# One full-width product for each expert's down-projection, order sums by accumulating transfers, and a new order of a VectorE step, in a fused attention and mixture-of-experts block

## What is computed

```python
# per batch row b: x 1024 x 256; sa, ca, ga, sb, cb, gb from silu(c) @ wmod
h = layernorm(x) * (1 + ca) + sa
q, k, v = split(h @ W_in.T)                       # 16 heads of 16
Tq, Tk = chebyshev(clip(q / 4)), chebyshev(clip(k / 4))        # 11 orders, 5 of them weighted
kv, ks = cumsum(Tk * v, tokens), cumsum(Tk.sum(-1), tokens)
out = (Tq * kv * beta).sum(orders) / ((Tq.sum(-1) * ks * beta).sum(orders) + 1e-7)
x = x + ga * (out @ W_out.T)
h = layernorm(x) * (1 + cb) + sb
w = sqrt(softplus(h @ routing_W.T + bias)) kept for the top 2 of 8 experts
x = x + gb * (shared(h) + sum_e w_e * (silu(h @ W1_e + b1_e) @ W2_e + b2_e))
```

## Time and profile before

| | us |
|---|---|
| median of 3 runs (lowest, highest) | 1087.46 (1085.91, 1087.97) |
| the profiled execution's own time | 1086.55 |
| its span, first to last instruction | 1084.9 |
| PE busy, DVE busy | 948.9, 947.9 |
| ACT busy, POOL busy | 472.5, 516.6 |
| step with p = 1 (465.9 to 526.2) | 60.3 |
| step with p = 0 (526.2 to 587.5) | 61.3 |

### The profile page before, as it was taken

How to read it: one execution, slowest core, us unless ns; L and a number is a source line. 1 busy time by engine, 2 the same in 40 slices (tenths; PEclk the granted TensorE clock), 3 DMA queues, 4 the chain that set the end, 5 groups by cost and what they waited for, 6 DMA issues and landing times.

```text
span 1084.9 us, 15500 instructions
## 1 busy us (share of the span) xinstructions
PE 948.9 (87%) x4889; PEld 678.4 (63%) x4889; DVE 947.9 (87%) x1465; ACT 472.5 (44%) x702; POOL 516.6 (48%) x615
## 2 busy tenths in 40 slices
PE   3864749998998989999999999898999999889996
PEld 3643436675756666675757576675757576656774
DVE  1498989999999999999999999999999999999432
ACT  4334335372635445362635444362635445441431
POOL 2032646646645546536645546536645445454210
PEclk9876869999999999999999999999999999999999
DMA  8100001020202002020202011020202010020211
GB/s 270 45 1 20 20 0 50 1 59 1 69 1 59 1 9 60 0 58 0 69 0 58 0 16 53 0 58 0 69 0 39 0 24 25 1 39 1 44 21 20
DMA packets 31517, 34.18 MB, mean 32 GB/s; under 512 B 1299, under 2 KB 30430, under 8 KB 31462
## 3 DMA queue, kind: packets, MB, share of 16 engines
q1 hardware_dynamic: 21410, 22.72, 6.3%
q0 software_dynamic: 8448, 8.39, 5.9%
q10 hardware_dynamic: 1604, 2.46, 0.7%
HBM read 16.77 MB, written 16.79 MB: 31 GB/s over the span
## 4 chain that ended last, share of the span: by engine, by line
PE 32%; DVE 30%; issue 18%; POOL 11%; ACT 3%; DVEq 1%; POOLq 0%; ACTq 0%
PE ring L1257 13%; PE acc L1394 7%; DVE feat L945 7%; PE tr L1342 4%; PE tr L1310 4%; DVE feat L966 3%; POOL feat L625 2%; DVE hid L1094 2%; DVE feat L962 2%; DVE feat L1004 2%; DVE feat L1001 2%; POOL ms L357 1%; PE tr L1248 1%; DVE route L1083 1%; PE cfb L1368 1%
## 5 line engine op out<-in xcount | busy, mean ns | idle before, releaser
L784 ACT ACTIVATE hid<-ring,b1row 128x512 f32<-128x512 f32 x144 | 98.6, 685 | 163.5 <-PE ring L1257 163.5
L630 POOL TENSOR_TENSOR feat<-feat 128x1024 f32<-128x1024 f32 x32 | 75.6, 2364 | 197.7 <-DVE feat L962 152.8
L1394 PE MATMUL acc<-w,hid 128*128 128x256 f32 x640 | 156.6, 392 | 0.0
L1394 PEld LDWEIGHTS acc<-w,hid 128*128 128x128 f32 x640 | 117.1, 191 | 28.0 <-issue 14.5
L945 DVE TENSOR_TENSOR_SCAN feat<-zero,carry,feat 128x512 f32<-128x512 f32 x80 | 113.1, 1453 | 0.0
L945 DVE TENSOR_TENSOR_SCAN feat<-zero,feat 128x512 f32<-128x512 f32 x80 | 109.9, 1413 | 0.0
L1094 DVE TENSOR_TENSOR hid<-hid,cfb 128x512 f32<-128x512 f32 x128 | 86.2, 673 | 25.7 <-PE cfb L1368 25.3
L1257 PE MATMUL ring<-n2H,w1H 128*128 128x512 f32 x288 | 101.9, 436 | 0.0
L1257 PE MATMUL ring<-n1H,winH 128*128 128x512 f32 x192 | 67.3, 433 | 38.7 <-ACT hid L784 24.9
L742 ACT ACTIVATE feat<-ring,bqkv 128x512 f32<-128x512 f32 x96 | 65.7, 686 | 71.5 <-PE ring L1257 71.5
L382 ACT ACTIVATE ntok<-xin,ms 128x256 f32 (+1 forms) x64 | 33.2, 589 | 138.5 <-POOL ms L361 138.5
(11 more groups left out here) (169 smaller groups left out, 2238.7 us busy)
## 6 DMA issues: line engine op xcount, KB each, us to landing
xin<-in_L_attn_x SPq DMA_DIRECT2D x16, 512.0 KB, 5.5
out<-x SPq DMA_DIRECT2D x16, 512.0 KB, 4.5
out<-fin POOLq DMA_DIRECT2D x16, 512.0 KB, 6.2
gates<-gate_rows SPq DMA_DIRECT2D x16, 128.0 KB, 4.8
feat<-in_L_wmod SPq DMA_DIRECT2D x1, 1536.0 KB, 14.1
feat<-in_L_attn_W_in SPq DMA_DIRECT2D x1, 768.0 KB, 9.5
const<-in_constants ACTq DMA_DIRECT2D x1, 690.5 KB, 4.3
fin<-in_constants ACTq DMA_DIRECT2D x1, 512.0 KB, 5.2
```

The lines of the kernel that those rows point to most:

```text
L630: g.tensor_tensor(f(W + 2 * n), f(W + 2 * n), f(W + 2 * n + 1), ALU.add).then_inc(added, 1)
L784: a.activation(hid[:, e % NG], ring[bank][:, :], ACT.Silu, bias=b1row[:, e:e + 1]).then_inc(ring_copied, 1)
L1394: last = mm(acc[t // 2][:, t % 2], x[:, t * P:(t + 1) * P], w[:, e // 2], start=False, stop=(e == E), skip_group_check=True)
```

## The change

1. All nine down-projections are one full-width float32 product for each token block; `w2` holds all nine weights, and `w2H`, `w2L`, `hidH`, `hidL`, ScalarE's four copies and VectorE's four subtractions of a step are gone.
2. The two GpSimd additions and one of the two VectorE additions of orders become three accumulating transfers from SBUF to SBUF (512 KB each, issued by GpSimd); the third waits for the first two, and VectorE's last addition waits for the third.
3. The order of VectorE's step is another, the carries are saved by three copies in place of five, `weigh(i, p, 3)` and `token_stats` come later, and the sums of order 4 before those of order 2.
4. On ScalarE the first normalisation and the squares of the next chunk change places; the powers on GpSimd move.
5. The softplus series has three instructions fewer.

```diff
-        w2 = sb("w2", [P, E // 2 + 1, D])
-        w2H = sb("w2H", [P, E // 2, D], f32r)
-        w2L = sb("w2L", [P, E // 2, D], f32r)
+        w2 = sb("w2", [P, NE, D])
...
                 c = number(i, p)
                 pool.wait_ge(odd_ready, 4 * c + 2)
-                ge(pool, numerator, 2 * c)
+                ge(pool, numerator, c)
                 g.tensor_tensor(f(W + 4), f(KT5), f(V0), ALU.mult).then_inc(weighted5, 1)
 
             def add_orders(i, p, n):
 
-                pool.wait_ge(products, ND * number(i, p) + 2 * n + 2)
-                g.tensor_tensor(f(W + 2 * n), f(W + 2 * n), f(W + 2 * n + 1), ALU.add).then_inc(added, 1)
+                c = number(i, p)
+                if n < 2:
+                    pool.wait_ge(products, ND * c + 2 * n + 2)
+                else:
+                    pool.wait_ge(added[0], 16 * c + 16)
+                    pool.wait_ge(added[1], 16 * c + 16)
+                into, of = ((W, W + 1), (W + 4, W + 3), (W, W + 4))[n]
+                pool.sem_inc(sum_begun, 1)
+                g.dma_start(f(into), f(of), accum_op=ALU.add).then_inc(added[n], 16)
...
                     add_orders(i, p, 0)
+                    add_orders(i, p, 1)
+                if st["second"]:
+                    exps(*later(i, p, -1))
+                if st["attn"]:
+                    add_orders(i, p, 2)
                 if st["norm"]:
                     inv_std(pool, 0, *later(i, p, 2))
                 if st["second"]:
-                    exps(*later(i, p, -1))
                     scores(*later(i, p, -1))
-                if st["attn"]:
-                    add_orders(i, p, 1)
-                if st["second"]:
                     split_weights(*later(i, p, -1))
                 if st["ffn"]:
...
                     act.wait_ge(clipped, 2 * c + q + 1)
+                    ge(act, summed, 2 * c - 1 + q)
                     if q == 0:
-                        ge(act, summed, 2 * c)
+                        ge(act, weighted, (ND - 1) * c)
+                        ge(act, weighted5, c)
+                    else:
                         ge(act, products, ND * c)
                     a.activation(f(s), f(x), ACT.Square).then_inc(squares, 1)
...
-                a.activation(hidH[:, :], hid[:, e % NG], ACT.Copy).then_inc(hidH_ready, 1)
...
-                if st["norm"]:
-                    normalise_first(act, *later(i, p, 2))
                 silu(5)
-                high(4)
                 copy("v0")
                 copy("v1")
                 silu(6)
+                if qkv:
+                    for which in range(3):
+                        square(*nxt, 0, which)
                 silu(7)
-                high(6)
+                if st["norm"]:
+                    normalise_first(act, *later(i, p, 2))
                 silu(8)
                 if qkv:
-                    for q in range(2):
-                        for which in range(3):
-                            square(*nxt, q, which)
+                    for which in range(3):
+                        square(*nxt, 1, which)
...
-            ORDERS = (0, 1, 3, 2, 4)
+            ORDERS = (0, 1, 3, 4, 2)
+
+            BY_WEIGHT = (0, 1, 3, 2)
+            NCARRY, CARRIED = 3, {0: 1, 1: 1, 3: 2, 4: 2, 2: 3}
...
+            def carry_over(i, p, k):
+
                 if p == 0:
-                    dve.wait_ge(scanned, ND * c + j + 1)
-                    v.tensor_copy(carry[:, n], feat[:, W + n, :, CT - 1]).then_inc(carried, 1)
+                    at, n, j = ((0, 2, 1), (3, 2, 3), (2, 1, 4))[k]
+                    dve.wait_ge(scanned, ND * number(i, p) + j + 1)
+                    v.tensor_copy(carry[:, at:at + n], feat[:, W + at:W + at + n, :, CT - 1]).then_inc(carried, 1)
...
-                dve.wait_ge(added, 2 * c + 1)
-                v.tensor_tensor(f(W), f(W), f(W + 4), ALU.add).then_inc(numerator, 1)
-                dve.wait_ge(numerator, 2 * c + 1)
-                dve.wait_ge(added, 2 * c + 2)
+                dve.wait_ge(added[2], 16 * c + 16)
                 v.tensor_tensor(f(W), f(W), f(W + 2), ALU.add).then_inc(numerator, 1)
...
-                for k, m in enumerate((11, 9, 7, 5, 3)):
-                    dve.wait_ge(soft_steps, at + 6 + k)
-                    v.scalar_tensor_tensor(out=b(PL), in0=b(PL), scalar=2.0 / m, in1=b(Z2),
+                v.scalar_tensor_tensor(out=b(PL), in0=b(Z), scalar=LOG1P[4], in1=b(Z),
+                                       op0=ALU.mult, op1=ALU.mult).then_inc(soft_steps, 1)
+                for k, m in enumerate((3, 2, 1)):
...
-                v.tensor_tensor(hidL[:, :], hid[:, e % NG], hidH[:, :].bitcast(f32), ALU.subtract).then_inc(hidL_ready, 1)
...
-                low(0)
                 if qkv:
                     lows(0, *nxt)
                 expert(1)
@@ -1137,49 +1112,51 @@
                 expert(2)
                 if attn_:
                     prefix(i, p, 1)
-                low(2)
+                if attn_:
+                    carry_over(i, p, 0)
                 if second:
                     lows(1, *prev)
                 if attn_:
                     order_product(i, p, 0)
                     order_product(i, p, 1)
                 expert(3)
+                if attn_:
+                    prefix(i, p, 2)
+                    prefix(i, p, 3)
+                expert(4)
+                if attn_:
+                    carry_over(i, p, 1)
+                    order_product(i, p, 2)
+                    order_product(i, p, 3)
+                if second:
+                    logit_parts(*prev)
+                if attn_:
+                    den_key_sums(i, p)
+                    den_products(i, p)
+                    weigh(i, p, 3)
                 if norm:
                     token_stats(dve, 0, *after2)
-                if attn_:
-                    weigh(i, p, 3)
-                    prefix(i, p, 2)
                 if qkv:
                     clip(*nxt, use, 0)
                     clip(*nxt, use, 1)
-                if second:
-                    logit_parts(*prev)
-                expert(4)
-                if attn_:
-                    den_key_sums(i, p)
-                    den_products(i, p)
-                low(4)
+                expert(5)
                 if second:
                     softplus(*prev)
                 if attn_:
-                    prefix(i, p, 3)
-                expert(5)
-                if attn_:
-                    order_product(i, p, 2)
-                    order_product(i, p, 3)
                     invert(i, p)
                 expert(6)
+                if attn_:
+                    prefix(i, p, 4)
+                if attn_:
+                    carry_over(i, p, 2)
+                    order_product(i, p, 4)
+                expert(7)
                 if second:
                     combine_weights(*prev)
-                low(6)
-                if attn_:
-                    prefix(i, p, 4)
-                expert(7)
-                if attn_:
-                    order_product(i, p, 4)
+                if attn_:
+                    finish_numerator(i, p)
                 expert(8)
                 if attn_:
-                    finish_numerator(i, p)
                     divide(i, p)
                 if ffn:
                     output(*exp)
...
-                if e in SPLIT:
-                    pe.wait_ge(hidL_ready, len(SPLIT) * c + e // 2 + 1)
-                    terms = ((hidH, w2H), (hidH, w2L), (hidL, w2H))
-                else:
-                    terms = ((hid[:, e % NG], w2),)
                 for t in range(NT):
-                    for x, w in terms:
-                        last = mm(acc[t // 2][:, t % 2], x[:, t * P:(t + 1) * P], w[:, e // 2], start=False,
-                                  stop=(e == E), skip_group_check=True)
+                    last = mm(acc[t // 2][:, t % 2], hid[:, e % NG, t * P:(t + 1) * P], w2[:, e], start=False,
+                              stop=(e == E), skip_group_check=True)
                 last.then_inc(expert_done, 1)
...
```

More of the change, by code:

```diff
@@ L14 @@
 K = 2
+LOG1P = (2.0000000076817583, 0.666663216413768, 0.40024595230747134, 0.2796515774481493, 0.2815777836368378)
 HID = 4 * D // E
@@ L169, in build @@
         hid = sb("hid", [P, NG, CT])
-        hidH = sb("hidH", [P, CT], f32r)
-        hidL = sb("hidL", [P, CT], f32r)
         fin = sb("fin", [P, NT, D])
@@ L240, in build @@
         products = sem("order_products")
-        added = sem("orders_added")
+        added = [sem(f"orders_added{n}") for n in range(3)]
+        sum_begun = sem("order_sums_begun")
         numerator = sem("numerator")
@@ L284, in build @@
         USES = len(RING)
-        SPLIT = range(0, E, 2)
         def number(i, p):
@@ L829, in step @@
                 silu(1)
-                high(0)
                 if qkv:
@@ L942, in prefix @@
                 if p:
-                    dve.wait_ge(carried, ND * i + j + 1)
+                    dve.wait_ge(carried, NCARRY * i + CARRIED[n])
```

(3 more changed lines are left out.)

47 lines of the change are left out of this document (12 added, 35 removed).

## The result

The changed kernel takes **1113.23 us** in the median of 4 runs (1110.17 to 1113.53), the kernel before 1086.68 us in the runs beside it (1085.52 to 1087.97). The ratio is 1.0238, with a 95% interval of 1.0215 to 1.026: 26.6 us slower. The profiled execution has a span of 1111.2 us, against 1084.9.

What follows compares the result with a forecast made beforehand. The prediction took VectorE to set the pace before the change and TensorE to be last after it. 13 x (1.0 stall + 1.45 clock) - 6.5 at the edges gave +25 us on 1086.55: 1112 us, range 1089 to 1124.

Steps and rivals of the forecast that it cites:

- The point that decides: Ahead of expert 6's up-projection, TensorE stands still 4.4 us for the copy of v0, held up by the last `weigh`.
- P to c: From the output projection's end to the start of `spread_weights` for expert 4: 30.9 us on TensorE.
- c to U: From `spread_weights` for expert 4 to expert 6's up-projection, start to start: 9.7 us (p = 0), 9.3 (p = 1).
- U to P: From the start of expert 6's up-projection to the output projection's end: 21.4 us on TensorE, before any clock loss.
- The clock: After TensorE's stall its clock falls, costing 1.7 us in 85% of the steps: 1.45 us a step.
- TensorE's own work: TensorE's work in a step without waits: about 56.2 us before the change, 57.6 us with it.
- Full-width products: Making a split expert's down-projection full costs TensorE 0.32 us, four times a step 1.3 us.
- Taken from VectorE: Four subtractions, one addition, three softplus steps and GpSimd's delay leave VectorE: about 4.8 us a step.
- Order sums by transfer: Three 512 KB transfers for each chunk, 6.2 us to each landing, ready before they are needed: cost nil.
- late-sums rival: Transfers within SBUF take 12 us, so the division comes 3 us late: about 1150 us, 8% chance.
- Edges: Setup, first two steps, the step without V copy and last two steps: together -6.5 us.
- faster rival: TensorE isn't held by V0, as VectorE's chain before the last `weigh` is shorter: 1056 us; 12% for any gain.

Runs made afterwards that it cites:

- e1: The changed kernel with VectorE's last `weigh` moved ahead of expert 4: 1039.49 us, ratio to the kernel before 0.9563.
- e2: The changed kernel with a second V buffer, one for each parity, and VectorE's order left as it was: 1052.19 us.
- e8: The changed kernel with the last `weigh` behind `logit_parts` and ahead of the denominator's sums: 1072.02 us.
- e9: The changed kernel with the last `weigh` ahead of `logit_parts`, behind `order_product(i, p, 3)`: 1053.28 us.
- e3: The changed kernel with 18 matmuls whose result nobody reads, put in the stall ahead of the up-projection of expert 6: 1087.17 us.
- e10: e1 with two more moves in VectorE's order, `token_stats` ahead of expert 4 and the inversion ahead of softplus: 1027.12 us.
- e11: e7 with the same two further moves in VectorE's order as e10: 1030.41 us.
- e7: e1 with the split down-projections of experts 0, 2, 4 and 6 put back: 1038.45 us.
- e5: The kernel before with nine full float32 down-projections and no splits, its order unchanged: 1067.35 us.
- e13: The kernel before with its two GpSimd additions as summing transfers at the same places, nothing else changed: 1071.78 us.
- e12: The changed kernel with its three summing transfers replaced by GpSimd additions: 1163.4 us.

## Why the prediction was right, and where its terms were not

*The point that decides.* Right. TensorE waits ahead of the up-projection of expert 6, for ScalarE's copy of v0, which waits for the last `weigh`; e1 and e2 take this away by two routes, and e8 and e9 grade it.

*The three pieces of a step.* Predicted for p = 0 and p = 1: P to c 30.9; c to U 9.7 and 9.3; U to P 21.4 and 1.45 for the clock. Measured in the changed kernel, p = 1: 627.02 - 596.33 = 30.7, 9.44, 659.86 - 636.46 = 23.4; p = 0: 30.7, 9.86, 22.2. The stall is 4.34 and 4.76 us for 4.0 and 4.4. The mean step became 63.2 us as predicted, and that closely by luck, because errors cancel:

- *The clock* was under-sized: 1.85 us in the mean (2.4 and 1.3) and in all 13 steps, for 1.45. e3 gives the same price.
- *TensorE's own work* was over-sized: 57.6 us a step, where e10 runs the same work without a wait in 56.43. Without the clock's loss U to P is 21.0 and 20.9 us, not 21.4, and P to c 30.7, not 30.9. The base was wrong, not what was added to it. I had taken the bracketed idle time of the kernel before for all that a wait costs, but from the products of experts 7 and 8 to the output projection it takes 584.24 - 579.01 = 5.23 us, in e10 548.95 - 545.39 = 3.56: 1.67 us for the 1.51 in the bracket. Waits too short for a bracket (0.15 us for `hidL` ahead of expert 2) were counted as work too, and the clock had cost 1.4 us there, not 1.3 (564.38 to 569.58 is 5.20 us; in the step from 647.8, where it held, 685.95 to 689.71 is 3.76).

*Full-width products* were priced right, at 0.32 us for 0.30 to 0.31 measured, but by luck: the two experts compared in the earlier trace rows are followed by different work. The kernel before has both kinds in a row in its last two steps, from `cfb` to `cfb` first split, then full:

```profile
1048.84 0.38 PE L1368 MATMUL cfb<-cfB,cfsel 25*128 25x512 bf16 x1
...
1052.17 0.38 PE L1368 MATMUL cfb<-cfB,cfsel 25*128 25x512 bf16 x1
...
1055.80 0.38 PE L1368 MATMUL cfb<-cfB,cfsel 25*128 25x512 bf16 x1
```

That is 3.33 us split and 3.63 full, 0.30 more. In full steps it is the same: from the first product of expert 0 to the second pair of matmuls behind it, e11 takes 505.11 - 503.12 = 1.99 us and e10 504.94 - 502.64 = 2.30. That the busy times of e10 and e11 differ by only 0.9 us a step doesn't speak against this: the modelled end of what runs ahead of a wait counts as busy, and e11 has four waits. My "corrected" 0.12 us in the expectation for e7 was wrong: with a full product ahead, the pair behind it takes 0.81 us (504.28 in e10) instead of 0.62, and start to start that pair had not been counted. The four passes of the Trainium skill (FP8 and Floating Point Precision, TensorE Precision Notes), 0.43 us for each expert by the estimate in the prediction, are not what these rows show.

*Taken from VectorE.* The 4.8 us a step are right (4.8 and 5.4). "This pays only where VectorE is late" is right too: e5 and e13 gain 19 and 15 us in the kernel before, where VectorE sets the pace.

*Order sums by transfer, "cost nil".* Their landing was over-sized (4.6 us for 6.2), and the late-sums rival fell. But "nil" named the cost and missed the worth: against additions on GpSimd at the same places they save 37 us in e1's order and 50 us in the changed one. I had costed GpSimd's interference from one row, L932 at 1.70 us, which is 0.24 us under its own mean over the span. The total was not hurt, since in the kernel before the additions lay elsewhere, and the steps were measured, not built up.

*Edges.* Predicted -6.5, measured: -3.3 to the first residual, -4.4 for the step behind it, 51.2 for 55.7 us in the step without V copies, and the tail 83.1 for 78.6: together -7.6. The tail is 4.5 us longer, three times what I gave; 8 x 0.30 is 2.4 of it, the rest isn't traced.

*The sum.* 13 steps give 976.92 - 151.63 = 825.3 us for 950.65 - 159.28 = 791.4: +33.9, less 7.6, is the +26.3 of the spans (predicted +25).

*The signs.* All but four came: a down-projection with its `cfb` takes 1.95 to 2.24 us, by what follows, not 2.15 throughout; PEclk is under 0.96 only with p = 1 (0.97 with p = 0), and VectorE's busy share is 83 to 85% in a step but 77% of the span, not 82%; and the steps with p = 0 last 62.6 to 62.9 us, not 63. The faster rival named the right lever, VectorE's stretch from c to U; its 1056 us for a freed V0 was too modest, e1 has 1039, in part for the same over-sized 57.6 us.

## What to carry to other kernels

A change that takes work from the busiest engine pays at its next wait, so look for the instruction that gives a buffer back and count what was put ahead of it: here one `weigh` behind 7 us of other work cost 74 us, while VectorE stood waiting just before. A stall on TensorE is priced with its clock, here 40% on top. And when GpSimd and VectorE work on the same memory, take VectorE's mean over the span for what GpSimd costs, and check where its instructions will fall in the new order; the same three additions cost 37 us in one order and 50 in another.

## What had not been expected of the hardware

- Matmuls that compute nothing of use shorten the run: 18 of them in each stall made the kernel 26.1 us faster (e3).
- After waits of 2.2 to 2.6 us the clock fell in seven steps of e8 and held in six, and the longer wait did not fall more surely; after 4.34 us it was low from the first matmul (1.22 us for a pair), and after 7.69 us (e12) the clock cost only 0.1 us more.
- A VectorE operation of 0.42 us took 2.57 us beside a GpSimd addition, till 0.28 us behind its end (e12).
- An accumulating transfer of 512 KB within SBUF lands in 4.6 us, sooner than the accumulating store to `out` (6.2 us), and cost VectorE nothing that shows.
